# Attention output kept with its columns on partitions, in a fused retention and FP4 feed-forward layer

## The chip, the cores and the metric

One core of a Trainium2 chip runs the whole layer as one program. The metric is device microseconds from start to end of one execution. TensorE (PE) multiplies, VectorE (DVE), ScalarE (ACT) and GpSimd (POOL) do everything between, SyncE (SP) issues most transfers. Each engine works through its own list of instructions in order, and they meet at semaphores. Names with `_ps` lie in PSUM, PE's output memory of eight banks, the others in SBUF.

## The reference

2048 tokens of 128 numbers pass a retention block with 8 heads (16 wide for q and k, 32 wide for v) and a feed-forward block whose operands are rounded to FP4 in blocks of 16; each block is followed by a residual sum and a layer norm.

```python
q, k = rope(x @ Wq), rope(x @ Wk)          # 8 heads of 16
v, g = x @ Wv, x @ Wg                      # 8 heads of 32
scores = einsum('bhqd,bhkd,hqk->bhqk', q * 16 ** -0.5, k, decay)   # decay is causal, per head
o = einsum('bhqk,bhkd->bhqd', scores, v)
o = o * rsqrt(mean(o * o, axis=-1) + 1e-5) * g_norm_w              # mean over the 32 of a head
x1 = layernorm(x + (o.reshape(b, l, 256) * silu(g)) @ Wo)
h = silu(fp4(x1) @ fp4(w_gate).T) * (fp4(x1) @ fp4(w_up).T)        # 352 wide
out = layernorm(x1 + fp4(h) @ fp4(w_down).T)
```

The decay is split into a factor for q and one for k (in the rotation tables) and a state that is carried from chunk to chunk, so that only a triangular mask is left within a chunk.

## The kernel before

The tokens are cut into 16 chunks of 128 (`C`). All matrices are f32. Every engine runs the same loop over stages `s`, and `run(step, ahead)` does `step` for chunk `s + ahead` if there is one; so a chunk passes through some ten stages, and one stage holds steps of many chunks. The order of the `run` lines of each engine is written out by hand as a table; nothing else sets it. The engines' stage counters are not tied to each other.

The path of one chunk through the attention half: PE projects q and k (`project_qk`, bank 4, L329) and v and g (`project_vg`, bank 5, one matmul of 512 columns, L338). DVE multiplies by the rotation tables (`rotate`), GpSimd adds the halves (`rotate_add`, L891), PE transposes q and k (`transpose_qk`, L346, L347), ScalarE copies them out (`q_even`, `q_odd`, `k_transposed`). PE forms the scores of 8 heads into banks 0 to 3, two heads in each (`scores`, L355, 32-row tiles of the array). `MB = 2`: the two first banks are masked by DVE straight from PSUM (`mask_scores` L748), the two others are copied by ScalarE to `raw` and masked by GpSimd (L895). PE multiplies the state with q into `oT_ps` (`from_state`, L385, banks 0 and 1), updates the state (`state_product`, L368, and DVE `next_state`), and adds the values (`values`, L395): the result `oT_ps` has the 256 columns of the attention output on partitions, in two halves, and the tokens in the free dimension.

From there the kernel turns it twice. ScalarE copies it out (`copy_oT`), PE transposes it so that tokens lie on partitions (`transpose_o`, L403, L404, bank 2), ScalarE squares it (`squares` L577), DVE sums the squares of each head (`mean_square` L765; a 33rd column holds EPS) and multiplies with silu(g) (`gated` L769), GpSimd takes the mean to the power -0.5 (`rms_rstd` L900) and multiplies (`gated_output` L905, into `y`). PE transposes `y` back (`transpose_y`, L411, L412, bank 3), ScalarE copies it (`copy_yT`), and PE projects with Wo (`out_projection`, L419, L420). Layer norm, FP4 rounding (`x_amax` to `x_value`), gate and up (L460, L467), FP4 rounding of h, three transposes (`transpose_h` L474), the down projection (`down` L483) and the second layer norm follow some stages later, on the same four engines. The FP4 rounding of the weights and their transposes are put into stages 0 to 3. `warm_up(n)` (L318) is n matmuls of the identity whose result nobody reads; 4 stand ahead of the loop and 4 after the first `project_qk`. In f32 a matmul of the program is two instructions in the trace and a transpose is one.

## Time and profile before

| | |
|---|---|
| median of 3 runs | 139.93 us (139.84 to 140.35) |
| profiled execution, its own time | 139.86 us |
| its span, first to last instruction | 137.9 us |
| busy PE, DVE, ACT, POOL | 122.2, 112.5, 98.2, 96.6 us |

The span is what the trace shows; 1.96 us of the execution's time lie around it. Busy time is the union of the recorded instructions of an engine. The granted clock is the share of full speed (2.4 GHz) that PE was given, where it is recorded. The transfers of inputs fill the first 20 us; afterwards only the outputs move. The kernel starts with the loads and the weights' rounding, then runs a steady pattern in which one chunk enters and one leaves in each stage, and drains when no new chunk is left.

### The profile page before, as it was taken

To read this page: it belongs to the slowest core of one execution; us is meant where nothing else is said; L and a number is where in the kernel's file an instruction comes from. 1 tells how busy PE (TensorE), PEld (TensorE's weight loads), DVE (VectorE), ACT (ScalarE), POOL (GpSimd) and SP (SyncE) were. 2 spreads that over 40 slices of the span, in tenths; PEclk is the share of its full clock that TensorE was granted. 3 is DMA by queue.
4 is the path that set the end of the run, shared out by engine and by line. 5 is a ranking of instruction groups with operands and counts; after the bars stand their busy time and mean duration, and the time that the engine had idled before them with its cause. 6 is when DMAs were issued, how large, how long until landed. Compare 5 with 4: busy or idle time off the path is not lost.

```text
span 137.9 us, 3502 instructions
## 1 busy us (share of the span) xinstructions
PE 122.2 (89%) x1224; PEld 78.1 (57%) x1224; DVE 112.5 (82%) x391; ACT 98.2 (71%) x311; POOL 96.6 (70%) x139
## 2 busy tenths in 40 slices
PE   4964998999999999999999999999999958888660
PEld 4822454657556465666667675757575735445550
DVE  1269468959778899999999999999999899999710
ACT  3055266678778796887888879797888978876763
POOL 4213727877876958888787979797979797656561
PEclk9999559999999999999999999999999999999997
DMA  3899980000000000000000000000000000000022
GB/s 116 255 250 233 412 257 8 0 5 5 0 5 0 0 5 2 0 5 2 0 0 5 0 2 24 0 19 7 19 0 19 5 19 19 19 21 19 19 59 60
DMA packets 6897, 6.53 MB, mean 47 GB/s; under 512 B 864, under 2 KB 6112, under 8 KB 6752
## 3 DMA queue, kind: packets, MB, share of 16 engines
q1 hardware_dynamic: 5856, 5.56, 13.6%
q10 hardware_dynamic: 1024, 0.76, 1.7%
q8 instruction: 10, 0.16, 0.5%
q14 instruction: 7, 0.06, 0.1%
HBM read 5.26 MB, written 1.05 MB: 46 GB/s over the span
## 4 chain that ended last, share of the span: by engine, by line
PE 78%; DVE 9%; ACT 7%; issue 2%; POOL 2%; POOLq 1%; ACTq 0%; DVEq 0%
PE ps L338 13%; PE ps L355 8%; PE ps L483 6%; PE ps L467 6%; PE ps L395 6%; PE ps L329 5%; PE ps L460 5%; PE ps L385 4%; PE ps L474 3%; PE ps L368 3%; PE ps L411 3%; PE ps L403 2%; PE ps L420 2%; PE ps L419 2%; ACT hT L513 2%
## 5 line engine op out<-in xcount | busy, mean ns | idle before, releaser
L900 POOL TENSOR_TENSOR rstd_h<-ms,minus_half 128x8 f32<-128x8 f32 x16 | 26.4, 1649 | 8.4 <-DVE ms L765 7.7
L891 POOL TENSOR_TENSOR qk<-rope_c,rope_s 128x256 f32<-128x256 f32 x16 | 11.6, 728 | 14.4 <-DVE rope_s L742 14.3
L338 PE MATMUL ps<-w_vg,xT_sb 128*128 128x512 f32 x32 | 19.0, 676 | 0.0
L483 PE MATMUL ps<-wd_T,hT 128*128 128x128 f32 x96 | 13.6, 278 | 2.7 <-ACT hT L513 2.7
L738 DVE TENSOR_TENSOR rope_c<-ps,tabs_sb 128x256 f32<-128x256 f32 x16 | 6.8, 424 | 11.1 <-PE ps L329 11.1
L925 POOL TENSOR_TENSOR hq<-h_grid,hs 128x352 f32<-128x352 f32 x16 | 13.0, 814 | 3.0 <-DVE h_grid L678 3.0
L514 ACT ACTIVATE q_eo<-ps,consts 128x128 f32<-128x128 f32 x32 | 11.8, 370 | 3.5 <-PE ps L347 3.5
L355 PE MATMUL ps<-q_eo,kT 32*128 32x256 f32 x128 | 12.0, 444 | 2.5 <-ACT q_eo L514 2.5
L483 PEld LDWEIGHTS ps<-wd_T,hT 128*128 128x128 f32 x96 | 12.1, 193 | 3.5 <-DVE r L792 2.6
L513 ACT ACTIVATE raw<-ps 128x512 f32<-128x512 f32 x16 | 9.6, 599 | 6.1 <-PE ps L355 6.1
L895 POOL TENSOR_SCALAR_AFFINE_SELECT probs<-raw 128x512 f32<-128x512 f32 x16 | 10.2, 637 | 5.0 <-ACT raw L513 5.0
L467 PE MATMUL ps<-wgu_T,xqT 128*128 128x352 f32 x32 | 12.4, 468 | 0.2
L748 DVE TENSOR_TENSOR probs<-ps,causal 128x512 f32<-128x512 f32 x16 | 10.9, 684 | 1.4 <-PE ps L355 1.3
L460 PE MATMUL ps<-wgu_T,xqT 128*128 128x352 f32 x32 | 12.1, 460 | 0.0
L513 ACT ACTIVATE v_sb<-ps 128x256 f32<-128x256 f32 x16 | 6.2, 385 | 7.5 <-PE ps L338 7.4
L911 POOL TENSOR_TENSOR rstd<-veps,minus_half 128x1 f32<-128x1 f32 x16 | 9.7, 606 | 2.2 <-DVE veps L781 2.1
L513 ACT ACTIVATE oT<-ps 128x256 f32<-128x256 f32 x16 | 6.2, 385 | 6.3 <-PE ps L395 5.3
L395 PE MATMUL ps<-probs,v_sb 128*32 128x128 f32 x256 | 10.5, 282 | 0.0
L329 PE MATMUL ps<-w_qk,xT_sb 128*128 128x256 f32 x32 | 10.5, 412 | 0.0
L915 POOL TENSOR_TENSOR rstd<-veps,minus_half 128x1 f32<-128x1 f32 x16 | 9.4, 591 | 1.4 <-ACT r_sq L612 1.4
L355 PEld LDWEIGHTS ps<-q_eo,kT 32*128 32x128 f32 x128 | 5.2, 190 | 8.7 <-issue 5.4
L919 POOL TENSOR_TENSOR xq<-x_grid,xs 128x128 f32<-128x128 f32 x16 | 7.5, 469 | 3.6 <-DVE x_grid L678 3.6
(112 smaller groups left out, 363.5 us busy)
## 6 DMA issues: line engine op xcount, KB each, us to landing
tabs_sb<-rope_tables SPq DMA_DIRECT2D x1, 1024.0 KB, 11.4
out<-x SPq DMA_DIRECT2D x16, 64.0 KB, 1.5
tabs_sb<-rope_tables SPq DMA_DIRECT2D x1, 640.0 KB, 8.0
xT_sb<-x_transposed SPq DMA_DIRECT2D x1, 512.0 KB, 9.4
x_res<-x SPq DMA_DIRECT2D x1, 512.0 KB, 12.0
xT_sb<-x_transposed SPq DMA_DIRECT2D x1, 320.0 KB, 6.6
x_res<-x SPq DMA_DIRECT2D x1, 320.0 KB, 8.6
w_vg<-in_w_vg ACTq DMA_DIRECT2D x1, 256.0 KB, 3.4
```

The lines of the kernel that those rows point to most:

```text
L329: mm(qk_ps, xT(c), w_qk[:], start=True, stop=True).then_inc(qk_pe, 1)
L338: mm(vg_ps, xT(c), w_vg[:], start=True, stop=True).then_inc(vg_pe, 1)
L355: last = mm(sc_ps(j), kT[rows, c % D, :], q_eo[rows, c % D, :, :].rearrange("p e q -> p (e q)"), start=True, stop=True)
L395: last = mm(oT_ps[32 * slot32:32 * slot32 + 32, n // 4, :], v_sb[:, c % D, n * DV:(n + 1) * DV], probs[:, c % 2, n, :], start=c == 0, stop ...
L460: mm(gate_ps, xqT[:, c % 2, :], wgu_T[:, 0:I], start=True, stop=True).then_inc(gate_pe, 1)
L467: mm(up_ps, xqT[:, c % 2, :], wgu_T[:, I:2 * I], start=True, stop=True).then_inc(up_pe, 1)
L483: last = mm(down_ps, hT[:, c % 2, t, :], wd_T[:, t, :], start=t == 0, stop=t == 2)
L513: copy = lambda o, i: nc.scalar.activation(o, i, ACT.Copy)
L514: scaled = lambda o, i, by: nc.scalar.activation(o, i, ACT.Identity, scale=by)
L891: gp.tensor_tensor(qk[:, c % D, :], rope_c[:, c % D, :], rope_s[:, c % D, :], ALU.add).then_inc(qk_p, 1)
L900: gp.tensor_tensor(rstd_h[:, c, :], ms[:, c, :], minus_half[:], ALU.pow).then_inc(rms_p, 1)
L925: gp.tensor_tensor(hq[:, c % 2, 0:I].rearrange("p (n k) -> p n k", k=BLK), h_grid[:, c % 2, :].rearrange("p (n k) -> p n k", k=BLK), hs[:, ...
```

## The change

Columns stay on partitions to the end. `squares` reads `oT_ps` directly and writes `o_sq` in the same orientation; the sum over a head's 32 rows is made by PE: `mean_squares` multiplies each half of `o_sq` (as the stationary operand, 128x128) with a 128x4 matrix of zeros and ones, `head_of_row`, which comes with four more columns of the constants. Its output, `ms_ps`, has tokens on partitions and 8 heads. DVE adds EPS while copying it out (`mean_square_eps`), GpSimd takes the power as before, ScalarE spreads the 8 numbers over 256 columns (`spread_rstd`, into `rstd_all`), and PE transposes that (`transpose_rstd`, bank 3). `gated` multiplies `oT_ps` with silu(g), and `gated_output`, now on DVE, multiplies with the transposed rstd, which gives `yT`. `copy_oT`, `copy_yT`, `transpose_o`, `transpose_y` and the old reduction are gone. So that silu(g) has columns on partitions too, `project_vg` is one matmul of 256 columns for v and two of 128 for g with the weights as stationary operand.

`MB = 0`: all four banks of scores are copied by ScalarE (one instruction of 128x1024) and masked by GpSimd (one of 128x1024); DVE masks nothing.

The scratch bank of `warm_up` is 6 instead of 7, and 4 warm-up matmuls follow `transpose_qk` of chunks 0, 1 and 2. All four order tables are written anew.

```diff
-MB = 2
+MB = 0
...
+        head_of_row = consts[:, 4:8]
...
             def project_vg(c):
...
-                mm(vg_ps, xT(c), w_vg[:], start=True, stop=True).then_inc(vg_pe, 1)
+                mm(v_ps, xT(c), w_vg[:, 0:VD], start=True, stop=True)
+                for g in range(2):
+                    last = mm(gT_ps[:, g, :], w_vg[:, VD + g * H:VD + (g + 1) * H], xT(c), start=True, stop=True)
+                last.then_inc(vg_pe, 1)
...
+                if c < 3:
+                    warm_up(4)
...
-            def transpose_o(c):
+            def mean_squares(c):
+
                 if tile[2] != "sc" or filled["sc"] > c + 1:
                     free_scores_bank(2)
...
+                pe.wait_ge(sq_act, c + 1)
+                for g in range(2):
+                    last = mm(ms_ps[:, 4 * g:4 * g + 4], o_sq[:, c % 2, g, :], head_of_row, start=True, stop=True)
+                last.then_inc(ms_pe, 1)
...
+            def transpose_rstd(c):
+
                 if tile[3] != "sc" or filled["sc"] > c + 1:
                     free_scores_bank(3)
...
+                pe.wait_ge(spread_act, c + 1)
+                for g in range(2):
+                    last = transpose(rstd_ps[:, g, :], rstd_all[:, c % 2, 4 * g:4 * g + 4, :].rearrange("p h d -> p (h d)"),
+                                     ident[:])
+                last.then_inc(rstd_pe, 1)
...
-            def copy_oT(c):
+            def squares(c):
                 act.wait_ge(o_pe, c + 1)
...
+                nc.scalar.activation(o_sq[:, c % 2, :, :], oT_ps, ACT.Square, scale=DV ** -0.5).then_inc(sq_act, 1)
+
+            def spread_rstd(c):
+
+                act.wait_ge(rms_p, c + 1)
+                copy(rstd_all[:, c % 2, :, :], rstd_h[:, c, :].unsqueeze(2).to_broadcast([C, NH, DV])).then_inc(spread_act, 1)
...
+            def mean_square_eps(c):
+                dve.wait_ge(ms_pe, c + 1)
+                vec.tensor_scalar(ms[:, c, :], ms_ps, EPS, None, ALU.add).then_inc(ms_v, 1)
...
+            def gated_output(c):
+                dve.wait_ge(gate_v, c + 1)
+                dve.wait_ge(rstd_pe, c + 1)
+                vec.tensor_tensor(yT[:, c % 2, :, :], gate_o[:, c % 2, :, :], rstd_ps, ALU.mult).then_inc(yT_v, 1)
```

On PE, in a full stage, from the values of one chunk to the scores of the next, before:

```order
L395 MATMUL ps<-probs,v_sb 32x128 x8
L411 MATMUL ps<-ident,y 128x128
L412 MATMUL ps<-ident,y 128x128
L452 MATMUL ps<-ident,xq 128x128
L483 MATMUL ps<-wd_T,hT 128x128 x3
L403 MATMUL ps<-ident,oT 128x128
L404 MATMUL ps<-ident,oT 128x128
L346 MATMUL ps<-ident,qk 128x128
L347 MATMUL ps<-ident,qk 128x128
L419 MATMUL ps<-wo_s,yT 128x128
L420 MATMUL ps<-wo_s,yT 128x128
L460 MATMUL ps<-wgu_T,xqT 128x352
```

and now (`consts` is `head_of_row`, L353 and L354 transpose q and k, L435 and L436 are the output projection, L499 down, L476 gate):

```order
L405 MATMUL ps<-probs,v_sb 32x128 x8
L468 MATMUL ps<-ident,xq 128x128
L353 MATMUL ps<-ident,qk 128x128
L354 MATMUL ps<-ident,qk 128x128
L435 MATMUL ps<-wo_s,yT 128x128
L436 MATMUL ps<-wo_s,yT 128x128
L416 MATMUL ps<-consts,o_sq 128x4 x2
L499 MATMUL ps<-wd_T,hT 128x128 x3
L476 MATMUL ps<-wgu_T,xqT 128x352
```

The four transposes of oT and y are gone, and the two narrow matmuls stand behind the transposes of q and k and the output projection.

On PE, the rest of the full stage, from the scores to the values, before:

```order
L355 MATMUL ps<-q_eo,kT 128x256 x4
L338 MATMUL ps<-w_vg,xT_sb 128x512
L474 MATMUL ps<-ident,hq 128x128 x3
L329 MATMUL ps<-w_qk,xT_sb 128x256
L385 MATMUL ps<-q_eo,S 32x128 x8
L368 MATMUL ps<-v_sb,qk 32x64 x4
```

and now:

```order
L364 MATMUL ps<-q_eo,kT 128x256 x4
L333 MATMUL ps<-w_qk,xT_sb 128x256
L342 MATMUL ps<-w_vg,xT_sb 128x256
L344 MATMUL ps<-xT_sb,w_vg 128x128 x2
L483 MATMUL ps<-wgu_T,xqT 128x352
L490 MATMUL ps<-ident,hq 128x128 x3
L426 MATMUL ps<-ident,rstd_all 128x128 x2
L394 MATMUL ps<-q_eo,S 32x128 x8
L377 MATMUL ps<-v_sb,qk 32x64 x4
```

The q/k projection has moved directly behind the scores; the up projection (L467 before, ahead of the scores) and the transposes of the spread rstd now stand between scores and values.

On PE, near the start, from the values of chunk 0 to the scores of chunk 1, before:

```order
L395 MATMUL ps<-probs,v_sb 32x128 x8
L403 MATMUL ps<-ident,oT 128x128
L404 MATMUL ps<-ident,oT 128x128
L346 MATMUL ps<-ident,qk 128x128
L347 MATMUL ps<-ident,qk 128x128
L355 MATMUL ps<-q_eo,kT 128x256 x4
```

and now (L327 is `warm_up`):

```order
L405 MATMUL ps<-probs,v_sb 32x128 x8
L353 MATMUL ps<-ident,qk 128x128
L354 MATMUL ps<-ident,qk 128x128
L327 MATMUL ps<-ident 128x128 x4
L416 MATMUL ps<-consts,o_sq 128x4 x2
L364 MATMUL ps<-q_eo,kT 128x256 x4
```

The warm-up block and the narrow matmuls fill the place between the transposes of q and k and the scores that wait for them.

## Rows read from the trace of the kernel before

**Rows 1.** Page, part 1: busy us, share of span, instructions.

```profile
PE 122.2 (89%) x1224; PEld 78.1 (57%) x1224; DVE 112.5 (82%) x391; ACT 98.2 (71%) x311; POOL 96.6 (70%) x139
```

**Rows 2.** Stretches: us, busy PE, PEld, DVE, ACT, POOL (instructions), PEclk, DMA, GB/s.

```profile
6.60:13.42 6.82, 4.05 (x42) 2.12 (x42) 5.05 (x16) 3.44 (x11) 1.36 (x2) 1.00 0.98 238
13.42:20.25 6.83, 6.53 (x55) 3.12 (x56) 4.12 (x9) 2.95 (x7) 3.61 (x4) 0.50 0.98 349
...
39.57:57.80 18.23, 18.08 (x205) 10.53 (x205) 16.84 (x63) 14.11 (x45) 13.82 (x20) 1.00 0.01 2
57.80:105.00 47.20, 47.20 (x537) 31.13 (x536) 45.02 (x163) 38.60 (x127) 39.85 (x55) 1.00 0.02 6
105.00:122.10 17.10, 14.31 (x110) 9.19 (x110) 16.50 (x63) 13.97 (x48) 13.15 (x20) 1.00 0.06 17
```

**Rows 3.** The chain of waits in order of time: start us, us, what.

```profile
13.72 1.25 PE ps L355 x8
...
21.87 0.72 PE ps L355 x8
...
27.85 0.64 PE ps L355 x8
...
38.97 0.59 PE ps L467 x2
39.57 0.64 PE ps L355 x8
```

**Rows 4.** Timeline of PE in one full stage: start us, us, engine, line, operation.

```profile
77.96 0.71 PE L355 MATMUL ps<-q_eo,kT 32*128 32x256 f32 x8
78.60 1.13 PE L338 MATMUL ps<-w_vg,xT_sb 128*128 128x512 f32 x2
79.57 0.49 PE L474 MATMUL ps<-ident,hq 128*128 128x128 f32 x3
...
80.93 0.62 PE L395 MATMUL ps<-probs,v_sb 128*32 128x128 f32 x16
81.48 0.33 PE L411 MATMUL ps<-ident,y 128*128 128x128 f32 x1
...
81.87 0.83 PE L483 MATMUL ps<-wd_T,hT 128*128 128x128 f32 x6
82.54 0.27 PE L403 MATMUL ps<-ident,oT 128*128 128x128 f32 x1
...
82.76 0.27 PE L346 MATMUL ps<-ident,qk 128*128 128x128 f32 x1
```

**Rows 5.** Timeline of the weight loads (PEld) in the same stage.

```profile
78.60 0.30 PEld L338 LDWEIGHTS ps<-w_vg,xT_sb 128*128 128x128 f32 x2 [0.33 <-issue]
...
81.48 0.14 PEld L411 LDWEIGHTS ps<-ident,y 128*128 128x128 f32 x1 [0.20 <-issue]
81.54 0.14 PEld L412 LDWEIGHTS ps<-ident,y 128*128 128x128 f32 x1
```

**Rows 6.** Who waited for whom: total us, times, longest us.

```profile
PEld ps L403 <- ACT oT L513: 2.8, 8, 0.8
```

**Rows 7.** Groups of instructions: busy us, mean ns of one | idle before.

```profile
L900 POOL TENSOR_TENSOR rstd_h<-ms,minus_half 128x8 f32<-128x8 f32 x16 | 26.4, 1649 | 8.4 <-DVE ms L765 7.7
...
L748 DVE TENSOR_TENSOR probs<-ps,causal 128x512 f32<-128x512 f32 x16 | 10.9, 684 | 1.4 <-PE ps L355 1.3
...
L895 POOL TENSOR_SCALAR_AFFINE_SELECT probs<-raw 128x512 f32<-128x512 f32 x16 | 10.2, 637 | 5.0 <-ACT raw L513 5.0
...
L513 ACT ACTIVATE raw<-ps 128x512 f32<-128x512 f32 x16 | 9.6, 599 | 6.1 <-PE ps L355 6.1
...
L765 DVE TENSOR_REDUCE ms<-o_sq 128x8 f32<-128x264 f32 x16 | 6.7, 418 | 1.6 <-ACT o_sq L577 1.5
...
L513 ACT ACTIVATE v_sb<-ps 128x256 f32<-128x256 f32 x16 | 6.2, 385 | 7.5 <-PE ps L338 7.4
...
L669 DVE SCALAR_TENSOR_TENSOR wr_ratio<-wgu_nat,wr_small 128x704 f32<-128x704 f32 x1 | 0.9, 879 | 0.0
```

## Prediction before the changed kernel was run

> **What bounds the kernel now.** I read the page's first part first: TensorE (PE) is busy 89% of the span, VectorE (DVE) 82%, the other two 70% [rows 1]. Such a mean says little, so the second view is the table of stretches, cut where the scores of chunks 5, 8 and 15 start [rows 2]. From 57.80 to 105.00 us PE is busy for all of its 47.20 us: seven stages of 6.74 us, in which every engine works and PE sets the pace. DVE has 45.02 us of busy time there, but neighbouring DVE instructions overlap in the records (the next starts up to 0.1 us before the last one's end), so its queue is really occupied about 6.5 of 6.74 us. From 39.57 to 57.80 us (no FFN-down work yet) three stages take 6.08 us each. From 105.0 to 122.1 us DVE is the full engine, 16.50 of 17.10 us. The start shows something else: from 13.42 to 20.25 us the granted clock is 0.50, the lower of PE's two levels (1.2 instead of 2.4 GHz). Just before, PE had work for only 4.05 of 6.82 us. The chain of waits, third view, gives the price [rows 3]: the scores of a chunk take 1.25 us at 13.72 and 0.64 us later, and the stage that begins at 13.72 ends at 21.87, after 8.15 us, where the next, to 27.85, needs 5.98.
>
> So there are three stretches with three limits: a start limited by waits and clock (0 to 39.57), ten stages limited by PE's instruction stream (to 105.0), and a drain limited by DVE and then by the round trip of the last chunks.
>
> **PE's stream in a full stage.** Starts are exact, ends are modelled, so I price by distances between starts [rows 4]. A transpose of 128 columns takes 0.11 us (the two of oT run from 82.54 to 82.76), a plain f32 matmul is two instructions of 0.11 each at 128 columns (six from 81.87 to 82.54), and the v/g projection with 512 columns takes 0.97 (78.60 to 79.57), of which some 0.10 is the change from the row-tiled scores to full-array work; the same change costs 0.06 in front of the transposes of y (81.48 to 81.87 holds three transposes, 0.39).
>
> Removed per stage: two transposes of oT and two of y, 0.44. Added: two transposes of the spread rstd, 0.22. The projection keeps its 512 columns but in three pieces (256, 128, 128), 4 x 0.11 + 2 x 0.22 = 0.88 against 0.87 without the change of mode: +0.02. Changes of mode stay as many as they were: scores, and the block from_state / state_product / values, stand between full-array work in both orders.
> The unknown is the mean of squares: two f32 matmuls, four instructions, that move only 4 columns over a full weight tile. No row shows one. Moving 4 columns is next to nothing, so what counts is how fast weights load. Two rows bound this [rows 5]: transposes' loads follow each other at 0.06 us (81.48, 81.54), those of a plain f32 matmul at 0.11 us (two of about 0.19 within 0.30 at 78.60). The squares are plain f32, so I take 4 x 0.108 = 0.43; the ends are 0.23 and, with a changed mode's 0.10 on top, 0.55. The Trainium skill says two things here ("TensorE: Matmul & The Clock Gate"). Section "LDWEIGHTS" gives the number of columns over 1.2 per ns, 107 ns for 128, whatever the rows; the trace agrees (0.11). Section "Back-to-back issue gap" puts 1 to 64 columns at a floor of about 25 ns each; as an estimate from that page the four would cost 0.10 and the final time would be some 3.3 us lower than mine. Its first rule has a row behind it here, the second has none.
> Sum for a full stage: -0.44 + 0.22 + 0.02 + 0.43 = **+0.23 us**, seven times: +1.6. In the three stages before that, PE today waits about 0.3 us per stage for the copy of oT in front of its transposes [rows 6]; that wait goes, since five instructions' worth of other work (0.83 us) now lies between the values and the mean of squares. There 6.98 - 1.00 (down 0.67, transposes of h 0.33) = 5.98 stands against 6.08: three times -0.1 = -0.3; with rounding, the ten stages give **+1.4**.
>
> **What moves on the other engines, and its cover** [rows 7]. DVE loses the mask (0.68) and the reduction over o_sq (0.42), and gains a multiply of 128x256 (between half the mask, 0.34, and that reduction, 0.42) and an add on 128x8 (about 0.1): 0.5 to 0.6 us less of 6.5. Nothing in the PE-bound stages gets shorter by it. ScalarE loses two copies of 128x256 (0.385 each, as v_sb) and gains one, while the copy of the scores grows from 512 to 1024 columns, 0.599 to 1.03 by the slope between 256 and 512: about even. GpSimd loses the multiply that made y, and its mask grows from 0.637 to some 1.1, at most 1.27 (twice): about even; its roots of the means, 1.65, stay.
> The growth lies on a path: scores, copy, mask, values. From the start of the scores: matmuls 0.72, ScalarE first finishes silu and norm (to about 0.9), copy 1.03, mask 1.1, handing over 0.1: values may start at 3.1 us. In PE's own stream the distance from scores to values is 2.97 today (77.96 to 80.93 [rows 4]); the up projection (0.59 [rows 3]) and the two rstd transposes (0.22) now stand in it as well, 3.8 us. So 0.7 us of cover in full stages, 0.4 without the transposes of h. The change therefore costs nothing there, but if the cover went, each 0.1 us would cost 1 us over ten stages. The other new round trip (squares, mean, GpSimd's root 1.65, spread 0.385, rstd transposes) has from 1 us to 5.9 us of the stage and needs about 3.2 us.
>
> **The start.** Stage by stage, from one chunk's scores to the next. First: values now wait for copy and mask of all heads, +0.3 us; but the q/k projection of the next chunk stands ahead of v/g, and the transposes behind the values no longer wait for a copy of oT, together -0.5: scores of chunk 1 at about 13.5 (13.72 today). Second: new is a block of four warm-up matmuls (8 x 0.11 = 0.9 us) after the transposes of chunks 0, 1 and 2. Those for chunks 0 and 1 fall where PE waits for ScalarE to copy q and k (part of the 2.8 us without work [rows 2]) and cost nothing. With PE's gaps filled I expect the clock to stay at its upper level. Then: scores 13.5; DVE's weight work, now ahead of the rotation of chunk 2 (one ratio of 0.88 us [rows 7], one of half the size, and five small steps, 2.5 us in all), holds it until 16.1, GpSimd's add ends at 17.7, transposes, warm-up 0.9, output projection 0.45, mean 0.43: scores of chunk 2 at 19.9, a stage of 6.4 instead of 8.15. Third: no warm-up, and the transposes of the gate/up weights (eight matmuls, about 1 us) have moved to the next stage: 5.2 instead of 5.98. Fourth and fifth, with all weight transposes: 12.15 instead of 11.72 (27.85 to 39.57). Chunk 5's scores start at 37.3 instead of 39.57: **-2.25**.
> The skill's section "The HAM clock gate" of the same page says that idleness takes the clock down and activity releases it; this trace agrees as far as the 0.50 after the idle stretch goes.
>
> **The drain.** Values of chunk 15 wait longer (3.8 against 2.97 after their scores), which the shorter round trip behind them (two copies and a transpose pair less, about 1 us) gives back. From there DVE is full, and it trades a reduction and a product for a product, an add and a product: **+0.1**. The last stages (two transposes, copy, down, sum) have the same order as before.
>
> Sum: 137.9 - 2.25 + 1.4 + 0.1 = 137.15 us of span. The profiled run took 139.86 with a span of 137.9, so 1.96 lie around it: **139.1 us**. Its time is 0.07 under the median of 139.93, within the spread of the three runs, and I add nothing for that.
>
> **The rivals.**
> (a) The clock falls all the same. For: PE keeps shorter waits around both stages, and the mean of squares leaves the array almost empty. Against: the two longest waits are filled. Price: the stage of 8.15 at the low level is my second stage without its warm-up, 5.5, and some 2.5 more: 141.6. It decides if a low stretch as long as today's begins before 20 us.
> (b) The mask path ends last, the mechanism that makes it slower even at full clock. All scores pass ScalarE, then GpSimd, one after the other; today half of them goes beside that through DVE. It decides once queueing ahead of the two exceeds 0.7 us (0.4 in the early stages); at 0.3 us beyond, ten stages cost 3 us: 142.1. Against: ScalarE has 38.60 and GpSimd 39.85 busy of 47.20 us [rows 2].
> (c) The narrow matmuls are cheap, 0.23: ten times -0.2 gives 137.1. For: weight loads 0.06 apart do occur; against: only for transposes [rows 5].
> (d) DVE's relief shortens the drain as well (it meets it 0.6 us per stage further ahead), 138.3; or the new order leaves small waits, 139.8. I count both into the forecast's own width, 138.2 to 140.1.
>
> **How the numbers follow.** Forecast 0.52, (a) 0.18, (b) 0.15, (c) 0.15. The range takes in (c) with a margin for its estimate and (a), and cuts through (b): 136.7 to 141.9; what is left out is about half of (b), the far side of (c) and surprises. A measurement of this kernel can tell about 0.5%, 0.7 us, from no change: faster means below 139.2. Of the forecast's width a bit over half lies there (0.29), 0.21 within, little above; with (c) 0.44 faster, 0.22 the same, and with (a) and (b) 0.34 slower.
>
> **What would show it.** Right: stretches of 6.97 us between scores in the second half; four weight loads 0.11 apart at the mean of squares; clock 1.00 from 6.6 us to the drain; chunk 5's scores near 37.3; PE's values with no wait on GpSimd's mask; DVE idle about 1 us per stage. Wrong: PE waiting for the mask or for the rstd transposes in every stage (b), a 0.50 in the first third (a), loads under 0.08 apart (c).

## The result, and the profile after

The changed kernel takes 139.99 us in the median of 20 executions (139.48 to 141.37); the kernel before, measured between them on the same chip, takes 139.04 us in the median of 20 (137.27 to 140.35). The ratio is 1.013, 95% interval 1.009 to 1.016: **slower by 1.3%**. This ratio leaves out the eight executions of the kernel before that took 139.84 us or more, over 1.5% above its fastest; of the two medians the ratio is 1.007. The forecast was 139.1 us and faster than the 139.93 us known then; its range, 136.7 to 141.9, holds the time, its sign is wrong.

The kernel before has no single time. These twenty executions come in three groups, near 137.3 (five), 139.0 (seven) and 140.1 us (eight), and the three that the forecast was made from (139.84 to 140.35) were all of the last group.

The profiled execution of the changed kernel took 140.44 us for a span of 138.0. First its page, parts 1 and 2, to be read against [rows 1]:

```profile
span 138.0 us, 3720 instructions
PE 125.4 (91%) x1344; PEld 92.8 (67%) x1344; DVE 103.9 (75%) x390; ACT 100.4 (73%) x295; POOL 98.1 (71%) x123
...
PEclk9999999999999999999999999999999999999998
```

VectorE (DVE) has 8.6 us less than before, TensorE (PE) 3.2 us more, and the clock is at its upper level in every slice. The stretches (us, busy PE, weight loads, DVE, ScalarE, GpSimd, clock, DMA share, GB/s), the first two cut as in [rows 2]:

```profile
6.60:13.42 6.82, 5.81 (x63) 4.82 (x63) 3.23 (x10) 3.77 (x10) 1.79 (x2) 1.00 0.98 243
13.42:20.25 6.83, 6.67 (x86) 5.34 (x84) 4.36 (x15) 4.33 (x11) 3.63 (x3) 1.00 0.95 345
...
60.00:105.00 45.00, 45.00 (x523) 33.88 (x519) 38.29 (x152) 36.89 (x112) 37.34 (x43) 1.00 0.03 8
105.00:122.00 17.00, 15.07 (x118) 10.00 (x110) 15.62 (x62) 13.73 (x45) 13.22 (x19) 1.00 0.04 13
```

From 13.42 to 20.25 us the clock is 1.00 where [rows 2] had 0.50. In the full stages PE is busy all the time and DVE has 0.85 of each us, as against 0.95 before. The chain of waits gives the starts of the scores, to be held against [rows 3] (13.72, 21.87, 27.85, 39.57):

```profile
13.77 0.98 PE ps L364 x8
...
19.99 0.96 PE ps L364 x8
...
25.35 0.77 PE ps L364 x8
...
37.49 0.64 PE ps L364 x8
```

(Starts in this chain lie up to 0.07 us behind those in PE's timeline; for chunk 3 before, it is 27.85 in the chain and 27.78 in the timeline, so the stage that [rows 3] gives as 5.98 us is 5.91.) So chunk 5 has its scores 2.1 us earlier than in the profile before, and still the two spans are equal: 137.9 and 138.0. The 2.1 us are given back in the ten stages and the drain. PE's timeline of one full stage, the counterpart of [rows 4]:

```profile
76.63 0.71 PE L364 MATMUL ps<-q_eo,kT 32*128 32x256 f32 x8
...
78.68 0.76 PE L483 MATMUL ps<-wgu_T,xqT 128*128 128x352 f32 x2
...
79.61 0.38 PE L426 MATMUL ps<-ident,rstd_all 128*128 128x128 f32 x2
...
80.43 0.62 PE L405 MATMUL ps<-probs,v_sb 128*32 128x128 f32 x16
...
81.59 0.39 PE L436 MATMUL ps<-wo_s,yT 128*128 128x128 f32 x2
81.81 0.51 PE L416 MATMUL ps<-consts,o_sq 128*128 128x4 f32 x4
82.18 0.91 PE L499 MATMUL ps<-wd_T,hT 128*128 128x128 f32 x6
...
83.61 0.71 PE L364 MATMUL ps<-q_eo,kT 32*128 32x256 f32 x8
```

The stage is 6.98 us from scores to scores (6.74 before), the values come 3.80 us after the scores with no wait in front, and the mean of squares, L416, holds the array for a good 0.4 us although it moves four columns. GpSimd's mask of the same chunk:

```profile
78.51 1.09 POOL L909 TENSOR_SCALAR_AFFINE_SELECT probs<-raw 128x1024 f32<-128x1024 f32 x1
```

It ends at 79.60, 0.83 us before the values start.

### The profile page after: what moved, and what is told of

The parts are those of the page before. It is cut to its first block, busy times and chain, and to the rows that moved or that the text cites. A ratio compares the mean times of both kernels' runs of the same rounds, so it can differ in the third digit from the quotient of the medians.

```text
span 138.0 us, 3720 instructions
## 1 busy us (share of the span) xinstructions
PE 125.4 (91%) x1344; PEld 92.8 (67%) x1344; DVE 103.9 (75%) x390; ACT 100.4 (73%) x295; POOL 98.1 (71%) x123
## 4 chain that ended last, share of the span: by engine, by line
PE 78%; DVE 9%; ACT 5%; POOL 3%; issue 3%; POOLq 1%; DVEq 0%; ACTq 0%
PE ps L364 8%; PE ps L333 7%; PE ps L499 6%; PE ps L483 6%; PE ps L476 5%; PE ps L405 5%; PE ps L344 5%; PE ps L342 5%; PE ps L394 4%; PE ps L416 4%; PE ps L490 3%; PE ps L327 3%; PE ps L377 3%; PE ps L426 2%; PE ps L468 2%
## 5 line engine op out<-in xcount | busy, mean ns | idle before, releaser
L909 POOL TENSOR_SCALAR_AFFINE_SELECT probs<-raw 128x1024 f32<-128x1024 f32 x16 | 17.6, 1101 | 6.6 <-ACT raw L529 6.1
L529 ACT ACTIVATE raw<-ps 128x1024 f32<-128x1024 f32 x16 | 16.4, 1025 | 4.1 <-PE ps L364 3.9
L499 PE MATMUL ps<-wd_T,hT 128*128 128x128 f32 x96 | 14.3, 285 | 2.7 <-ACT hT L529 2.7
L918 POOL TENSOR_TENSOR rstd<-veps,minus_half 128x1 f32<-128x1 f32 x16 | 10.3, 647 | 8.7 <-DVE veps L795 8.7
L499 PEld LDWEIGHTS ps<-wd_T,hT 128*128 128x128 f32 x96 | 12.1, 193 | 3.5 <-DVE r L806 2.6
L922 POOL TENSOR_TENSOR rstd<-veps,minus_half 128x1 f32<-128x1 f32 x16 | 11.3, 707 | 3.9 <-ACT r_sq L623 3.9
L824 DVE TENSOR_TENSOR h_blocks<-ps,silu_h 128x352 f32<-128x352 f32 x16 | 8.4, 523 | 7.3 <-PE ps L483 7.2
L588 ACT ACTIVATE o_sq<-ps 128x256 f32<-128x256 f32 x16 | 6.2, 384 | 10.2 <-PE ps L405 10.2
L476 PE MATMUL ps<-wgu_T,xqT 128*128 128x352 f32 x32 | 12.4, 471 | 0.0
L529 ACT ACTIVATE hT<-ps 128x384 f32<-128x384 f32 x16 | 7.9, 491 | 5.9 <-PE ps L490 5.8
L333 PE MATMUL ps<-w_qk,xT_sb 128*128 128x256 f32 x32 | 11.5, 444 | 0.0
L604 ACT ACTIVATE silu_h<-ps 128x352 f32<-128x352 f32 x16 | 7.4, 463 | 5.4 <-PE ps L476 4.9
L344 PEld LDWEIGHTS ps<-xT_sb,w_vg 128*128 128x128 f32 x64 | 9.7, 191 | 0.8
```

Source lines behind the costliest of these rows:

```text
L333: mm(qk_ps, xT(c), w_qk[:], start=True, stop=True).then_inc(qk_pe, 1)
L344: last = mm(gT_ps[:, g, :], w_vg[:, VD + g * H:VD + (g + 1) * H], xT(c), start=True, stop=True)
L476: mm(gate_ps, xqT[:, c % 2, :], wgu_T[:, 0:I], start=True, stop=True).then_inc(gate_pe, 1)
L499: last = mm(down_ps, hT[:, c % 2, t, :], wd_T[:, t, :], start=t == 0, stop=t == 2)
L529: copy = lambda o, i: nc.scalar.activation(o, i, ACT.Copy)
L909: gp.affine_select(out=probs[:, c % 2, 2 * MB:, :], in_=raw[:, c % 2, :, :], compare_op=ALU.is_ge, fill=0.0, base=0, pattern=[[0, NH - 2 * ...
```

## Experiments: is the gain at the start real?

The first theory was the forecast's own: the block of warm-up matmuls takes away a low-clock stretch that costs 2 to 3 us, always. The rival: the low stretch is an accident of the profiled execution, so that the gain is there only in some executions.

**The kernel before, once more, with nothing edited.**

> The kernel before, unchanged, to see span and granted clock of each execution. Clock theory: the stretch at the lower clock near 13 us is in some executions and not in others; executions with a mean clock near 1.0 have a span near 135.5 us (137.3 us of time), those with 0.97 near 137.9 (139.9). Rival (the spread lies around the span, in launch and end): spans all within 0.5 us of 137.9 whatever the time, clock the same in all.

Its twelve executions have a median of 139.97 us. Spans and mean granted clocks go together: three at 135.3 to 135.6 us with a clock of 1.00, two at 137.0 and 137.1 with 0.987 and 0.988, seven at 138.0 to 138.6 with 0.966 to 0.975. The profile fell on one of the middle group. Its stretches, the second one cut at the low part:

```profile
6.59:14.00 7.41, 4.34 (x46) 2.25 (x46) 5.39 (x17) 3.68 (x11) 1.68 (x3) 1.00 0.97 241
14.26:17.67 3.41, 3.41 (x12) 1.20 (x7) 1.43 (x3) 1.23 (x4) 2.30 (x3) 0.50 1.05 417
17.68:21.08 3.40, 2.69 (x51) 1.79 (x51) 3.16 (x8) 2.96 (x9) 1.01 (x2) 1.00 0.73 225
```

and what PE does there:

```profile
13.97 1.03 PE L355 MATMUL ps<-q_eo,kT 32*128 32x256 f32 x8 [1.09 <-ACT q_eo L514]
14.93 2.08 PE L338 MATMUL ps<-w_vg,xT_sb 128*128 128x512 f32 x2
16.79 1.03 PE L329 MATMUL ps<-w_qk,xT_sb 128*128 128x256 f32 x2
...
21.08 0.72 PE L355 MATMUL ps<-q_eo,kT 32*128 32x256 f32 x8 [0.57 <-ACT q_eo L514]
21.73 1.13 PE L338 MATMUL ps<-w_vg,xT_sb 128*128 128x512 f32 x2
```

The same projection takes 1.86 us to the next start at 14.93 and 0.97 at 21.73. Here the low stretch lasts 3.41 us, half of the 6.83 of [rows 2], and the stage from chunk 1 to chunk 2 is 7.11 us instead of 8.15. Every other stage has the length that it had before (5.91 or 5.92, 5.72, 6.00, three of 6.08, seven of 6.74). So the low stretch comes whole or half in the same program; that it is missing in the executions at a clock of 1.00 follows from that clock, no profile caught one. PE was busy for 4.05 of 6.80 us before the whole stretch and for 4.31 before the half one (6.60 to 13.40 us), and what decides between the two no run here shows.

The clock does not explain every long execution either. Of 68 more executions of this kernel, measured beside the edited ones, eight have spans of 140.1 to 140.3 us at a mean clock of 0.990 to 0.991, which is 4.8 to 5.0 us above the fastest with hardly any low clock, and one has 147.4 us at 0.833. No profile caught one of these; their cause stays open.

**Four warm-ups in the kernel before, after the transposes of q and k of chunks 0 and 1 alone.**

```diff
-            def warm_up(n):
+            def warm_up(n, bank=7):
...
-                    mm(ps[:, 7, 0:C], ident[:], ident[:], start=True, stop=True)
+                    mm(ps[:, bank, 0:C], ident[:], ident[:], start=True, stop=True)
...
                 fill(4, "qkT")
+                if c < 2:
+                    warm_up(4, 6)
```

> The kernel before with four warm-up matmuls (scratch bank 6) behind the transposes of q and k of chunks 0 and 1, where PE waits anyway. Clock theory: mean clock 0.99 or more in every execution, span 135.3 to 136 us, so about 137.4 us, 1.2% faster than the median of before. Rival (the warm-ups don't hold the clock, or cost what they bring): times spread as before's, median 139 or more.

137.35 us in the median of nine, 137.27 to 137.66, clock 0.992 to 0.998: ratio 0.992 [0.988, 0.996]. None of the nine is in a slower group. The stretches now read:

```profile
6.60:13.40 6.80, 5.72 (x58) 4.08 (x58) 4.96 (x16) 3.34 (x11) 1.36 (x2) 1.00 0.96 250
13.40:20.25 6.85, 5.86 (x73) 3.37 (x73) 6.09 (x15) 4.49 (x14) 4.80 (x5) 1.00 0.97 348
```

The second stage is 5.55 us. The best spans are those of the unedited kernel's best executions, 135.3 us, so these two blocks cost nothing in the old order: the stage with the first block is as long as without it (5.60 and 5.61 us), since the block stands in the wait for ScalarE. This is the kernel before at full clock, and what the change has to be compared with.

**The changed kernel without its blocks.**

```diff
                 fill(4, "qkT")
-                if c < 3:
-                    warm_up(4)
```

> The changed kernel without its twelve extra warm-up matmuls. Clock theory: part of the executions get a lower clock near 13 us and take 1.5 to 2.5 us longer (141 or more), the others lose the 0.9 us block of chunk 2 from the path: 139.1. Rival (the mean of squares and the earlier projection fill the gaps enough): all executions at clock 0.99 and at 139.1.

Five executions at 138.13 to 138.16 us (span 136.4, clock 0.997 or 0.998), 1 us below the 139.1 expected, five at 139.51 to 139.69 (137.8 and 137.9, 0.981 to 0.985), two at 141.23 and 141.69 (0.970, 0.960); median 139.55, ratio 1.002 [0.997, 1.008]. So the new order without warm-ups is open to a low stretch as well. At full clock it needs 136.4 us, 1.1 more than the old order. The profile, which shows 1.00 throughout, has stages of 5.16, 5.33 and 5.18 us, and the scores of chunk 5 start at 35.84 us; in the old order at full clock (two blocks, by the same view) they start at 36.98. The new order is 1.1 us ahead there and loses more than that behind it.

**The changed kernel with the blocks of chunks 0 and 1 alone** (`c < 2` for `c < 3`).

> The changed kernel with warm-ups after the transposes of chunks 0 and 1 only. If the block of chunk 2 lies on the path, as I reckoned (0.9 us), and the first two hold the clock: 139.1 us, 0.9 below the changed kernel's 140.0, clock 0.99 or more. Rival (in stage 1 DVE's weight work holds everything, so the block is hidden): no difference, 140.0.

138.83 us in the median of twelve (138.57 to 139.66), clock 0.991 to 1.000, spans mostly 136.8 to 137.0; ratio 1.001 [0.998, 1.004]. Against the changed kernel, with spans from 137.7 us up, the third block costs 0.9 us: its stages of 6.22 and 5.43 us become 5.58 and 5.17. Against no block at all (136.4) the first two cost 0.4 to 0.6 (chunk 5's scores at 36.44 instead of 35.84). They are not free here: in this order PE has other work to fill the wait for ScalarE's copies.

```profile
18.03 0.27 PE L354 MATMUL ps<-ident,qk 128*128 128x128 f32 x1
18.14 1.06 PE L327 MATMUL ps<-ident 128*128 128x128 f32 x8
19.04 0.39 PE L435 MATMUL ps<-wo_s,yT 128*128 128x128 f32 x2
...
19.48 0.51 PE L416 MATMUL ps<-consts,o_sq 128*128 128x4 f32 x4
19.92 1.03 PE L364 MATMUL ps<-q_eo,kT 32*128 32x256 f32 x8
```

This is the changed kernel's PE before the scores of chunk 2. Between the transposes and the scores stand the block (0.90), the output projection (0.44) and the mean (0.44) without a gap, 1.78 us in all. Without the blocks the same piece takes 1.13, and PE waits for ScalarE's copies:

```profile
17.46 0.39 PE L433 MATMUL ps<-wo_s,yT 128*128 128x128 f32 x2
...
17.90 0.51 PE L414 MATMUL ps<-consts,o_sq 128*128 128x4 f32 x4
18.59 0.78 PE L362 MATMUL ps<-q_eo,kT 32*128 32x256 f32 x8 [0.18 <-ACT q_eo L528]
```

At full clock, then, the lowest spans are 135.3 (before), 136.4 (changed, no block), 136.8 (two blocks), 137.7 us (three). The rival holds for the clock: the 2 to 3 us that the blocks were to save are there only when the kernel before falls into the low stretch. The new order by itself gains 1.1 us at the start, the three blocks take 1.6 (35.84 to 37.42), and the change without any block costs 1.1 us over the whole span.

## Experiments: where the full stage grew

The following edits are made to the version with two blocks, whose full stage is 6.99 us and whose lowest span is 136.8 us. The theory: the narrow matmuls cost four weight loads of 0.11 us, whatever they move. The rivals: it is the columns or the matmul itself; or the growth is a wait on the mask.

**128 columns moved instead of four.**

```diff
-                    last = mm(ms_ps[:, 4 * g:4 * g + 4], o_sq[:, c % 2, g, :], head_of_row, start=True, stop=True)
+                    last = mm(ps[:, 2, g * C:(g + 1) * C], o_sq[:, c % 2, g, :], ident[:], start=True, stop=True)
```

> The changed kernel with two warm-up blocks (138.8 us), but the two matmuls of the mean move 128 columns (the identity) instead of 4; the means are then not the means. If the load of the f32 weight tile (0.11 us) is the cost: a stage stays at 6.99 and the time at 138.8 (at most 0.1 more, since the last matmul's columns now stand before the next one), that is, 4 columns cost what 128 do. Rival (part of the cost grows with the columns): 0.05 us or more for each of four instructions, 7.2 us a stage, 141.

Full stages of 6.99 us, as before the edit; the median of ten is 139.30 us, 0.5 more than the 138.83 of its base, where at most 0.1 was expected. The lowest spans, 137.3, are 0.5 longer; about half of that shows in the third and fourth stage (5.28 for 5.17, 6.16 for 6.01); why was not taken apart. One of the ten took 655.91 us, at a clock of 1.00, for which nothing here gives a cause. So 32 times as many columns are free where PE is the bound. The groups of both kernels, loads first:

```profile
L416 PEld LDWEIGHTS ps<-consts,o_sq 128*128 128x128 f32 x64 | 8.4, 192 | 0.0
```

```profile
L416 PEld LDWEIGHTS ps<-ident,o_sq 128*128 128x128 f32 x64 | 8.4, 192 | 0.0
```

The mean duration of the loads is the same to the ns (they overlap: the four start 0.11 us apart, 81.70 to 82.15 in the changed kernel, where the next weights follow). The columns are ruled out by this run. That it is the loads, and not another fixed price of an f32 instruction on the full array, is the reading of these records; the bf16 run below changes both together.

**The squares and the matrix of zeros and ones in bf16** (the squares are rounded, the sums stay f32).

```diff
-        head_of_row = consts[:, 4:8]
+        head_of_row = sb("head_of_row", 128, 4, dt=bf16)
...
-        o_sq = sb("o_sq", 128, 2, 2, C)
+        o_sq = sb("o_sq", 128, 2, 2, C, dt=bf16)
...
+            pool.wait_ge(d_cst, 16)
+            gp.tensor_copy(head_of_row[:], consts[:, 4:8]).then_inc(c_ident, 1)
```

> As the changed kernel with two warm-up blocks (138.8 us), but the squares and the 0/1 matrix are bf16, so that the mean is two instructions instead of four. If the loads of the weights, 0.11 us each in f32, are the whole cost of the narrow matmuls: at least two of four go, -0.22 us a stage, up to -0.35 if a bf16 tile loads in 0.06 or less: 135.6 to 136.9. Rival (fixed cost per matmul with 4 columns, loads hidden): less than 0.1 us a stage, 138 or more.

134.34 us in the median of four (134.17 to 135.17), ratio 0.963 [0.958, 0.967]: the fastest kernel here, and below the 135.6 to 136.9 that was expected. Against the kernel before at full clock (137.35 us) it is 2.2%. A bf16 product is one load and one matmul instead of two of each. Groups, then PE's timeline:

```profile
L416 PEld LDWEIGHTS ps<-head_of_row,o_sq 128*128 128x128 bf16 x32 | 3.1, 99 | 0.2
```

```profile
78.86 0.19 PE L416 MATMUL ps<-head_of_row,o_sq 128*128 128x4 bf16 x2
78.92 0.36 PE L499 MATMUL ps<-wd_T,hT 128*128 128x128 f32 x1
```

Two products take 0.06 us from start to the next work's start, against 0.37 for the four f32 instructions (81.81 to 82.18 above). The full stage is 6.68 us, 0.31 less, below the 6.74 of the kernel before, and the stages ahead of it are 5.77 instead of 6.08. Ten stages give 3.1 us; the spans fell by 4.4 (136.8 to 132.4). The rest lies in the fourth and fifth stage (6.01 and 6.07 to 5.75 each, 0.6) and in the drain (33.4 to 33.0 from the scores of chunk 15), with the first stages' scatter. What was expected counted the ten stages only.

The Trainium skill has both halves of this. "TensorE: Matmul & The Clock Gate", section "Weight-path perf modes — Fast Weight Load (FWL) and DoubleRow", says that 128 weights in a type other than FP32 are loaded in a faster way; this trace agrees, 0.03 us per bf16 product against 0.11 per f32 load. Its section "Back-to-back issue gap", weighed in the prediction, holds a floor of about 25 ns for up to 64 columns: the bf16 products come near it, the f32 ones do not. The same section says that in a stream of loads and matmuls both set the spacing, which the prediction left out when it priced its estimate.

**The same kernel again.**

> The changed kernel with two warm-up blocks and bf16 squares once more, for its interval: 134.3 us, 0.966 of the kernel before in executions of the same state, clock 0.99 or more in all. If its four executions so far were lucky in the clock: some near 136 to 137.

Four of six executions lie between 134.19 and 135.20 us; ratio 0.973 [0.965, 0.980]. The fifth took 136.57 us, with a span of 134.8 and a clock of 0.980, so the expected 0.99 in all was missed and two blocks do not keep the low clock away for certain; the sixth took 282.68 us at a clock of 1.00, unexplained. The profiled execution has a span of 132.4 us. The stages are the same from the third on (5.14, 5.75, 5.75, three of 5.77, seven of 6.68); the first is 5.16 us where the other profile had 6.00. The gain is confirmed.

**One transpose of the spread rstd instead of two.**

```diff
-                for g in range(2):
+                for g in range(1):
```

> As the changed kernel with two warm-up blocks (138.8 us), but only the first of the two transposes of the spread rstd is made, and both halves of the output are multiplied with it: one 128-column transpose of PE's work per chunk is left out. If PE's stream sets the stage: 6.98 becomes 6.87, seven times, some less in the three earlier stages: 137.9. Rival (another engine ends last): no change, 138.8.

137.65 us (137.61 to 137.85), full stages of 6.88 us: 0.11 for a transpose, seven times, as [rows 4] had priced it. The lowest span is 135.9, 0.9 below its base: 0.8 from the full stages, 0.1 from the fifth. The three stages of 6.08 us do not move: there PE's state product, which comes behind this transpose, waits for DVE anyway (shown below, in the part on the prediction).

**DVE masks two banks again** (`MB = 2`, with `mask_scores` of the next chunk ahead of the rotation).

```diff
-MB = 0
+MB = 2
...
+                run(mask_scores, 1)
                 if s == 0:
                     weights_ratio(0)
```

> The changed kernel with warm-ups for chunks 0 and 1 only (138.8 us), and half of the scores masked by DVE again (behind h_ratio), as in the kernel before. My reckoning (copy and mask of all scores are covered by 0.4 to 0.7 us of PE's stream): stages stay at 6.98 and 6.08 us; only chunk 0's values, which wait for the mask at the start, come 0.3 us earlier, 138.5. Rival (mask path ends last in the stages): 0.1 us or more off each of ten stages, 137.8 or less.

141.45 us in the median of four (140.45 to 142.63), ratio 1.010 [1.003, 1.017]; neither the expectation nor its rival had it slower. Full stages stay at 6.99 us, so in the PE-bound part it does not matter who masks. The first four stages are 6.26, 6.45, 6.45 and 6.60 instead of 5.35, 5.58, 5.17 and 6.01, since DVE's mask now stands, beside the rounding of the weights, ahead of the rotation of the chunk after next:

```profile
15.45 0.69 DVE L757 TENSOR_TENSOR probs<-ps,causal 128x512 f32<-128x512 f32 x1
16.05 0.88 DVE L679 SCALAR_TENSOR_TENSOR wr_ratio<-wgu_nat,wr_small 128x704 f32<-128x704 f32 x1
...
16.85 0.96 DVE L679 SCALAR_TENSOR_TENSOR wr_ratio<-wd_nat,wr_small 128x352 f32<-128x352 f32 x1
...
19.41 0.33 PE L353 MATMUL ps<-ident,qk 128*128 128x128 f32 x1 [0.93 <-POOL qk L906]
```

The rotation follows at 17.73 us (15.99 in its base, where the scores of chunk 1 are 0.76 us earlier). PE waits for GpSimd's `qk` 3.1 us in all. One stretch at the low clock (mean 0.75 from 20.25 to 27.10 us) is in that profile too, though the two blocks are in this kernel, and a second of the four executions has a clock of 0.988. The executions with clocks of 0.993 and 0.999 have spans of 138.5 and 139.0 us, 1.7 to 2.2 above their base, and that part is not the clock's. So the relief of DVE does nothing for the full stages and about 2 us for the start of this order.

**The up projection back ahead of the scores.**

```diff
                 run(gate, -4)
+                run(up, -4)
                 run(scores, 1)
                 run(project_qk, 2)
                 run(project_vg, 1)
-                run(up, -4)
```

> As the changed kernel with two warm-up blocks (138.8 us), but PE does the up projection ahead of the scores, as the kernel before. Reckoning: the 0.1 us wait of the state product for DVE's product of h goes in the three stages before the down work (6.08 to 5.98), -0.3; but the cover of the mask path shrinks by 0.59 to 0.1 in full stages and below zero (-0.2) in those three, +0.6: 139.1 in all, with PE waiting for the mask in the early stages. Rival (the cover was larger than reckoned): 138.5.

140.65 us in the median of ten (140.18 to 141.40), clearly more than expected; lowest span 138.4, 1.6 above its base. The stages say where: 6.66 instead of 6.07 once, 6.30 instead of 6.08 three times, 7.04 instead of 6.99 seven times: 0.59 + 0.66 + 0.35 = 1.6. The 0.59 is the first up projection itself, which now falls ahead of chunk 5's scores. The rest looks like the mask that was expected, but the trace says otherwise. A full stage (scores, mask, values, and the weights of the up projection at its end):

```profile
62.87 0.71 PE L364 MATMUL ps<-q_eo,kT 32*128 32x256 f32 x8
...
64.75 1.09 POOL L909 TENSOR_SCALAR_AFFINE_SELECT probs<-raw 128x1024 f32<-128x1024 f32 x1 [1.19 <-ACT raw L529]
...
66.08 0.62 PE L405 MATMUL ps<-probs,v_sb 128*32 128x128 f32 x16
...
69.12 0.30 PEld L483 LDWEIGHTS ps<-wgu_T,xqT 128*128 128x128 f32 x2 [0.35 <-DVE r L806]
```

The values start 3.21 us after the scores, which is the 3.80 of the changed kernel less the up projection, and 0.24 us after the mask's end: they do not wait. The additional 0.05 us lies at the up projection, whose weights wait for the sum `r` with which DVE frees its bank. In the three stages of 6.30 us the mask ends 0.21 us before the values too (46.19 and 46.40); there PE starts the transposes of rstd 0.20 us later than its own stream would, 0.1 us behind the end of ScalarE's spread, which follows its copy of the scores. So even without the up projection the values do not wait for the mask. In full stages 0.24 us of cover are left; in the three others the mask ends 2.96 us after the scores, and without PE's other waits the values would come at about the same time. The expectation was wrong about the cause and about the size.

## Experiment: the drain

From the scores of chunk 15 to the end the kernel before takes 33.0 us and the changed one 33.4. DVE's waits from 104 to 122 us, before (with 0.3 us for `x_blocks` beside it):

```profile
DVE ms L765 <- ACT o_sq L577: 0.2, 1, 0.2
```

and changed:

```profile
DVE h_blocks L824 <- PE ps L483: 1.1, 1, 1.1
DVE ms L774 <- PE ps L416: 0.2, 1, 0.2
```

DVE's wait for the mean stands in front of the whole rounding of h. If that is what costs, it helps to put the mean behind it in the last stages:

```diff
-                run(mean_square_eps, 0)
+                if s < 15:
+                    run(mean_square_eps, 0)
...
                 run(h_plus_, -6)
...
+                if s >= 15:
+                    run(mean_square_eps, 0)
```

> As the changed kernel with two warm-up blocks (138.8 us), but in the last stage that has a mean, stage 15, DVE does h_plus ahead of the copy of the means. If DVE's waits for the mean on PE (0.2 to 0.5 us near 108) are what the drain lost against the kernel before: 138.4 to 138.6. Rival (the drain is limited by chunk 15's own round trip through GpSimd, which now starts later): 138.8 or more.

138.94 us in the median of ten, against 138.83: nothing. In its profile the wait for the mean is 0.3 us elsewhere: DVE waits that long for the down projection, which stands behind the mean on PE. The other wait is 1.1 us long, for the up projection, which now stands behind the scores: `h_blocks` starts 2.41 us after the scores of chunk 15 (104.58 to 106.99), and 1.73 before. In the run with the up projection ahead of the scores that wait is gone, but DVE waits 1.4 us for the transposes of rstd instead, and from scores to end it is 33.2 us. With the squares in bf16 `h_blocks` is as late (2.42 us after the scores) and yet the drain is back at 33.0. So the late `h_blocks` alone does not cost the 0.4 us; a cheaper mean on PE gives them back. What holds this drain besides was not taken apart. DVE's wait in that run, same stretch:

```profile
DVE yT L783 <- PE ps L426: 1.4, 1, 1.4
```

## Why the prediction was wrong

**The step that failed is the start's -2.25 us**, above all the number that it was subtracted from. The changed kernel's start did what was said: scores of chunk 1 at 13.8 (13.5), of chunk 2 at 20.0 (19.9), of chunk 5 at 37.49 (37.3), clock 1.00 throughout. But "8.15 us" for the second stage of the kernel before [rows 2, 3] was one of three values that this stage takes with the clock: 8.15, 7.11 and, with the clock up, 5.55 (this one read from the kernel with two blocks). The stretch at 0.50 was read as a property of the kernel, from one execution; the spread of three runs that agreed within 0.5 us gave no hint. With the clock up, the scores of chunk 5 start at 36.98 us (the kernel before with two blocks), and the changed kernel's are 0.4 us later (37.42 by the same view), not 2.1 earlier: the new order gives 1.1 us, the three blocks take 1.6. Rival (a) had the low stretch coming back in the changed kernel; the case of the kernel before losing it by itself was missing from the rivals.

**That is half of the miss.** A gain of 0.83 us was forecast (139.1 against 139.93) and by the medians 0.95 us were lost. Of these 1.78 us, 0.89 are the kernel before, whose median fell from 139.93 to 139.04 us once twenty executions were taken. The other 0.89 are the changed kernel itself, 139.99 instead of 139.1: in the profiled span 138.0 instead of 137.15, of which 0.2 lie in the start, 0.3 in the ten stages and 0.3 in the drain. Even against the 139.93 us known then, there was no gain.

**Two free blocks.** "Those for chunks 0 and 1 cost nothing" holds in the old order and not in the new one (0.4 to 0.6 us at full clock), where the projection and the mean already fill the wait. The third block was priced at 0.9 and measured 0.9. That it might be spared was not weighed; with two, none of nine executions in the old order and none of twelve in the new one had a low stretch (clocks of 0.991 and more), but one of ten with bf16 squares and two of four with DVE's mask had a clock of 0.988 or less.

**The ten stages, +1.4, measured +1.7.** From the scores of chunk 5 to those of chunk 15 it is 67.16 us, and 65.43 before. The full stage is 6.99 against a forecast of 6.97, and the parts that were measured alone came as priced: a transpose 0.11, the mean's four instructions 0.44. Rival (c), cheap narrow matmuls, falls for f32. The miss is in the three stages before: 6.08, not 5.98. The wait for the copy of oT did go, as said, but the stage still has a short wait, in another place:

```profile
46.35 0.53 DVE L824 TENSOR_TENSOR h_blocks<-ps,silu_h 128x352 f32<-128x352 f32 x1 [0.65 <-PE ps L483]
...
46.93 0.16 PEld L377 LDWEIGHTS ps<-v_sb,qk 128*32 128x32 f32 x8 [0.29 <-DVE h_blocks L824]
```

The profile puts PE's state product behind DVE's product `h_blocks`, which waits for the up projection: the state product starts 0.47 us after `from_state`, and 0.38 in a full stage, and the 0.09 are the miss. A matmul that is moved back moves its readers too, and what is queued behind them; the prediction followed PE's side of that move only.

**The mask path.** The copy of 128x1024 measured 1025 ns (1.03 said) and the mask 1101 (1.1 said). From scores to the mask's end it is 2.97 us (3.1 said), so the cover is 0.83 us in full stages and 0.60 in the three before (46.47 to 47.07), where 0.7 and 0.4 were reckoned. Rival (b) did not come about.

**The drain, +0.1, measured +0.4.** The prediction let a shorter round trip give back the later values, and gave the mean on PE no price here. With the bf16 mean, 0.31 us cheaper a stage, the drain takes 33.0 us again; `h_blocks`, late by 0.7 us through the up projection, is so in both. Which step carries the 0.4 us was not followed further.

Together at full clock: +0.44 (start), +1.73 (ten stages), +0.43 (drain) are the 2.6 us between the spans of 135.4 and 138.0 us. Measured medians differ by only 0.95 us because fifteen of the twenty executions of the kernel before are in its two slower groups (1.5 to 3.1 us above its fastest; where the clock of such an execution is on record, it is 0.965 to 0.988), and none of the changed kernel's twenty has a clock under 0.99.

## What to carry to other kernels

Before a stretch at the low clock is counted as a cost, look at the granted clock and span of every execution: if they come in groups, the stretch belongs to some of them, and a change has to be set against the best group. Here a handful of spare matmuls in waits that PE had anyway made the low stretches rare; once other work filled those waits, the same matmuls were a cost. The reduction that was given to PE cost 0.44 us in f32 whatever it moved, and 0.31 less in bf16. And a run that comes out slower, as expected, still has to be looked at: with the up projection ahead of the scores the mask was expected to be the limit, and it was not.

## What was not expected of the hardware

- One program: with four spare matmuls in each of two waits its nine executions lie between 137.27 and 137.66 us, without them twelve lie between 137.26 and 140.56.
- An f32 product with a stationary operand of 128x128 holds PE for two times 0.11 us, with 4 as with 128 columns moved; a bf16 product with 4 columns for 0.03 us.
- The start scatters by itself as well. In the run with 128 columns the first stage was 6.64 us instead of 5.35. There DVE's reduction of the down weights started at 9.51 us, after a wait of 3.7 us for their transfer (3.2 in others), and the step behind it, on 128x22 numbers, took 1.04 us instead of 0.18; the rotation of chunk 1 is queued behind both (at 11.37 us). GpSimd's first mask runs from 9.98 to 11.07 us, and the small step ends 0.03 us after it. The same is seen in three more profiles of the new order, with first stages of 6.00 to 6.26 us: a small step of this kind that starts during the mask takes 0.55 to 0.84 us and ends 0.03 us after the mask. In the other six these steps start before the mask and take 0.11 to 0.18 us. A reciprocal that starts during the mask takes its usual 0.29 us. So a transfer that lands a little later puts this step of DVE behind one of GpSimd.

```profile
9.51 0.52 DVE L671 TENSOR_REDUCE wr_small<-wd_nat 128x22 f32<-128x352 f32 x1 [3.74 <-DMA wd_nat<-in_w_down]
9.98 1.09 POOL L909 TENSOR_SCALAR_AFFINE_SELECT probs<-raw 128x1024 f32<-128x1024 f32 x1 [3.41 <-ACT raw L529]
10.06 1.04 DVE L705 TENSOR_SCALAR wr_small<-wr_small 128x22 f32<-128x22 f32 x1
```
